# Value blocks as sequences of their own, and the first two sums of the last decoder as a piece of their own

## What is computed

```
# layer 0
xn = layernorm(x)
x = x + channel_attention(xn) + experts(xn)      # 64 experts, top 8, and a shared one
# layer 1
xn = layernorm(x)
x = x + sparse_attention(xn) + bitlinear_ffn(xn)

def sparse_attention(x):                         # per head h of 8, width 16
    q_h = relu(x @ enc_q[h]);  v_h = relu(x @ enc_v[h])
    metric = softplus(base + 0.1 * (gelu(signal(q) @ w1 + b1) @ w2 + b2))
    # each query looks at the 64 tokens up to itself
    dist = sqrt(((k_window - q_h) ** 2 * metric).sum(-1) + 1e-8)
    topd, loc = top_k(-dist, 32)
    infl = exp(-topd);  infl /= infl.sum() + 1e-8
    context = einsum(infl, v_h[loc])
    context += gate * 0.1 * (q_h / norm(q_h)) @ (hebb_U[h] @ hebb_V[h])
    return (q_h * context for all h) @ decoder
```

## Time and profile before

| | us |
|---|---|
| median of 3 runs (680.79 to 680.95) | 680.8 |
| the profiled execution | 682.07 |
| its span | 680.3 |
| PE busy | 642.2 (94%) |
| DVE busy | 550.7 (81%) |
| ACT busy | 444.3 (65%) |
| POOL busy | 367.6 (54%) |
| mean granted clock of TensorE | 0.988 |

### The profile page before, as it was taken

The page is one execution under the profiler, slowest core; times in us unless marked ns, Lnnn a source line. Parts: engine busy times, 40 slices in busy tenths (PEclk is TensorE's granted clock), DMA queues, the critical chain, the costliest instruction groups (busy, mean ns, idle before and its releaser), DMA issues.

```text
span 680.3 us, 14252 instructions
## 1 busy us (share of the span) xinstructions
PE 642.2 (94%) x4792; PEld 435.5 (64%) x4792; DVE 550.7 (81%) x2461; ACT 444.3 (65%) x802; POOL 367.6 (54%) x448
## 2 busy tenths in 40 slices
PE   4888999999999999999999999999999999998785
PEld 3555765667556666766666567666657766675674
DVE  5998688746967999997986999984477999937996
ACT  3675454646687868557688877446879855478762
POOL 2288366646363688755463895665653577511220
PEclk9999899999999899999999999999999999999898
DMA  8930000000000000000000000000000000000000
GB/s 299 402 116 1 0 1 0 1 0 1 0 1 1 2 2 1 1 1 1 2 0 2 2 2 1 1 1 1 1 1 2 2 1 1 1 17 2 18 17 17
DMA packets 12968, 15.81 MB, mean 23 GB/s; under 512 B 1728, under 2 KB 10832, under 8 KB 12384
## 3 DMA queue, kind: packets, MB, share of 16 engines
q1 hardware_dynamic: 12896, 14.91, 6.3%
HBM read 13.85 MB, written 1.05 MB: 22 GB/s over the span
## 4 chain that ended last, share of the span: by engine, by line
PE 70%; DVE 18%; ACT 5%; POOL 3%; issue 3%; DMA 0%; DVEq 0%; POOLq 0%; ACTq 0%
PE bank_A L523 19%; PE bank_G L523 16%; PE bank_U L523 16%; PE bank_X L523 16%; DVE Wk L1269 4%; DVE m L1266 3%; DVE S L850 2%; DVE GWk L850 2%; PE bank_X L816 1%; PE bank_X L532 1%; ACT Ed L1336 1%; ACT L1341 1%; POOL PR L1643 1%; POOL Wlo L1643 1%; ACT L1336 1%
## 5 line engine op out<-in xcount | busy, mean ns | idle before, releaser
L1643 POOL TENSOR_TENSOR Wlo<-Wgu,Whi 128x256 fp32r<-128x256 f32 x184 | 136.2, 747 | 135.1 <-ACT Whi L1336 134.3
L523 PE MATMUL bank_A<-S,WdT 128*128 128x512 f32 x346 | 171.4, 598 | 0.2 <-POOL S L1643 0.2
L850 DVE TENSOR_TENSOR S<-S,bank_U 128x512 f32<-128x512 f32 x173 | 116.6, 682 | 35.1 <-PE bank_U L523 21.3
L1643 POOL TENSOR_TENSOR S<-S,Rb 128x512 f32<-128x512 f32 x84 | 109.3, 1302 | 56.4 <-DVE S L850 55.9
L523 PE MATMUL bank_G<-xH,Whi 128*128 128x512 f32 x184 | 99.6, 541 | 4.5 <-POOL Wlo L1643 2.3
L1336 ACT ACTIVATE Whi<-Wgu 128x256 fp32r<-128x256 f32 x184 | 73.4, 412 | 40.8 <-PE bank_U L523 36.1
L523 PE MATMUL bank_U<-xH,Whi 128*128 128x512 f32 x184 | 96.7, 525 | 0.1
L523 PEld LDWEIGHTS bank_A<-S,WdT 128*128 128x128 f32 x346 | 62.7, 190 | 33.9 <-issue 23.3
L1269 DVE MATCH_REPLACE8 Wk<-m,Wk 128x79 f32<-128x79 f32 x384 | 82.1, 225 | 0.0
L1336 ACT ACTIVATE S<-bank_G 128x512 f32<-128x512 f32 x90 | 53.6, 596 | 43.1 <-PE bank_G L523 37.9
L850 DVE TENSOR_TENSOR S<-Rb,bank_G 128x512 f32<-128x512 f32 x83 | 56.3, 679 | 25.6 <-ACT bank_G L1336 20.0
(11 more groups left out here) (294 smaller groups left out, 1184.9 us busy)
## 6 DMA issues: line engine op xcount, KB each, us to landing
Wgu<-in_Wgu SPq DMA_DIRECT2D x2, 2048.0 KB, 14.2
xs<-in_x SPq DMA_DIRECT2D x4, 256.0 KB, 6.0
wqk<-in_w_qkv SPq DMA_DIRECT2D x1, 1024.0 KB, 7.2
Wgu<-in_Wgu SPq DMA_DIRECT2D x1, 1024.0 KB, 8.9
out<-xs SPq DMA_DIRECT2D x3, 256.0 KB, 2.3
Wgu<-in_Wgu SPq DMA_DIRECT2D x1, 512.0 KB, 5.1
wout<-in_w_out SPq DMA_DIRECT2D x1, 512.0 KB, 7.7
wvT<-in_wvT SPq DMA_DIRECT2D x1, 512.0 KB, 8.5
```

The costliest lines, as they stand in the source:

```text
L523: return engine.matmul(dst, lhsT, rhs, start=start, stop=stop)
L850: return engine.tensor_tensor(dst, a, b, op)
L1643: return engine.tensor_tensor(dst, a, b, op)
```

## The change

**Value blocks.** V0 and V1 leave `head` on PE and on ACT and become sequences of their own, `values(b)`, with the letters k on PE and v on ACT. In the banks they stand behind pq: in X2 for the batches 0 to 2, in U1 for the last one. There is no other work in them than before.

**Decoder.** Of the four products of a decoder sum in the last batch the first two, x·ident and hq·dec, become steps of their own, `decode_early`, with the letter x on PE. They count up a semaphore `dec_x`, for which `decode` waits before its two cc products.

**Order.** The strings of PE, DVE, ACT and POOL are written anew nearly throughout. No matmul and no other instruction is added or taken away. Lines of the changed kernel stand one less (523 is 522) up to the first hunk of PE, and 9 to 11 more behind it.

```diff
@@ uses()
-        for what in ("v0", "v1"):
-            add("U1" if last else "X2", what, b)
         for what in ("bdq", "hbm"):
             add("U0" if last else "X2", what, b)
-        add("U1" if last else "X2", "pq", b)
+        for what in ("pq", "v0", "v1"):
+            add("U1" if last else "X2", what, b)
@@ tensor engine
+            def values(b):
+                yTb = yT_of(b)
                 for k in range(2):
                     yield
                     t = fill(f"v{k}", b)
...
@@ decode(b, i)
-                t, c, h = fill("dec", b, i), cc[i % 2], slice(128 * i, 128 * i + 128)
-                pe.wait_ge("hq", 1)
-                if i < FIRST:
-                    pe.wait_ge(empty(bank("mo", b)), nth("mo", b) + 1)
-                else:
-                    pe.wait_ge(empty(bank("ff2", b)), nth("ff2", b) + 1)
-                mm(t[:, 0:128], ident, xb(b)[:, i, :], True, False)
+                t, c = ps("dec", b, i), cc[i % 2]
+                pe.wait_ge("dec_x", i + 1)
                 u = 2 * i + 1 + (i == NT - 1)
                 pe.wait_ge(empty(bank("ctx", b, u)), nth("ctx", b, u) + 1)
-                mm(t[:, 0:128], hq[:, h], dec[:, :], False, False)
                 mm(t[:, 0:128], c[:, 0, :], dec[:, :], False, False)
                 mm(t[:, 0:128], c[:, 1, :], dec[:, :], False, True).then_inc(sems(full(bank("dec", b, i))), 1)
+
+            def decode_early(b):
+
+                for i in range(NT):
+                    yield
+                    t = fill("dec", b, i)
+                    pe.wait_ge("hq", 1)
+                    if i < FIRST:
+                        pe.wait_ge(empty(bank("mo", b)), nth("mo", b) + 1)
+                    else:
+                        pe.wait_ge(empty(bank("ff2", b)), nth("ff2", b) + 1)
+                    mm(t[:, 0:128], ident, xb(b)[:, i, :], True, False)
+                    mm(t[:, 0:128], hq[:, 128 * i:128 * i + 128], dec[:, :], False, False).then_inc(sems("dec_x"), 1)
@@ weave
-                  h=heads(), d=every(distances), t=every(turns))
+                  h=heads(), k=every(values), d=every(distances), t=every(turns), x=decode_early(B - 1))
```

More of the change, by code:

```diff
@@ L44 @@
     "pe":
[L45 to L49, removed]
@@ L726, in head @@
                 mm(t[:, :], encq[:, :], yTb[:, :]).then_inc(sems(full(bank("enc", b))), 1)
-                for k in range(2):
-                    yield
-                    t = fill(f"v{k}", b)
-                    pe.wait_ge(empty(bank("y", b)), nth("y", b) + 1)
-                    for i in range(NG // 2):
-                        at = 64 * (NG // 2 * k + i) - 64
-                        o = slice(128 * i, 128 * i + 128)
-                        if at < 0:
-                            mm(t[0:64, o], yTb[:, 0:1].to_broadcast([128, 64]), encv[:, :])
-                            mm(t[64:128, o], yTb[:, 0:64], encv[:, :])
-                        else:
-                            p = mm(t[:, o], yTb[:, at:at + 128], encv[:, :])
-                    p.then_inc(sems(full(bank(f"v{k}", b))), 1)
                 yield
@@ L768, in head @@
                 p.then_inc(sems(full(bank("pq", b))), 1)
+            def values(b):
+                yTb = yT_of(b)
+                for k in range(2):
+                    yield
+                    t = fill(f"v{k}", b)
+                    pe.wait_ge(empty(bank("y", b)), nth("y", b) + 1)
+                    for i in range(NG // 2):
+                        at = 64 * (NG // 2 * k + i) - 64
+                        o = slice(128 * i, 128 * i + 128)
+                        if at < 0:
+                            mm(t[0:64, o], yTb[:, 0:1].to_broadcast([128, 64]), encv[:, :])
+                            mm(t[64:128, o], yTb[:, 0:64], encv[:, :])
+                        else:
+                            p = mm(t[:, o], yTb[:, at:at + 128], encv[:, :])
+                    p.then_inc(sems(full(bank(f"v{k}", b))), 1)
             def distances(b):
@@ L1523, in head @@
                 act(ksq[:, :], kp[:, PADK:], ACT.Square).then_inc(sems("ksq"), 1)
-                for k in range(2):
-                    yield
-                    t = filled(f"v{k}", b)
-                    if b > 0:
-                        q = NG // 2 * k + NG // 2 - 1
-                        sc_.wait_ge(full(bank("ctx", b - 1, q)), nth("ctx", b - 1, q) + 1)
-                    emptied(act(V[:, NG // 2 * k:NG // 2 * k + NG // 2, :],
-                                t[:, :].rearrange("p (g c) -> p g c", g=NG // 2), ACT.Relu), f"v{k}", b)
                 yield
@@ L1564, in head @@
                     ACT.Copy).then_inc(sems("pk"), 1)
+            def values(b):
+                for k in range(2):
+                    yield
+                    t = filled(f"v{k}", b)
+                    if b > 0:
+                        q = NG // 2 * k + NG // 2 - 1
+                        sc_.wait_ge(full(bank("ctx", b - 1, q)), nth("ctx", b - 1, q) + 1)
+                    emptied(act(V[:, NG // 2 * k:NG // 2 * k + NG // 2, :],
+                                t[:, :].rearrange("p (g c) -> p g c", g=NG // 2), ACT.Relu), f"v{k}", b)
             def operands(b):
@@ L1634, in scalar_engine @@
             weave("act", x=highs(), e=silus(), m=sums(), y=every(route), s=every(spreads), c=scales(), u=setup(),
-                  a=every(attend), f=every(dense), h=every(head), o=every(operands), k=every(keys), n=every(near), g=every(gather), q=ends())
+                  a=every(attend), f=every(dense), h=every(head), v=every(values), o=every(operands), k=every(keys), n=every(near), g=every(gather), q=ends())
         def gpsimd_engine(engine):
```

54 lines of the change are left out of this document (30 added, 24 removed).

## The result

The changed kernel takes 679.4 us by the median of 22 runs (677.9 to 681.4), the kernel before, over its own 22 runs, 681.0 (678.9 to 683.3). The ratio is 0.998, with a 95% interval of 0.997 to 0.9989: faster by 0.2%, some 1.4 us, where 4.6 us (676.2) were forecast with 679.0 as the upper bound. The two profiled executions show more, 682.07 and 678.06 us. The granted clock tells most of it.

The account below looks back on a forecast made before the run. Bounds: PE in the expert loop, a cross-engine chain in the last batch's head, DVE in its top-k, then the last chain. Terms −3.75 −0.43 −0.5 −0.3 +0.4 = −4.6 off 680.8 gave 676.2 us, range 673.4 to 679.0.

Parts of the forecast that it names:

- A: Last products of the expert loop: turn 2.6 moves behind the last two downs, PE still does not wait; −0.45 us.
- B: Last sums up to the keys: the last batch's ln starts when its input is ready; −0.85 us more.
- E: Head of the last batch: V0 in its new place on PE, between PQ and the first distances, costs +0.6 us.
- F: End of the kernel: first decoder products done early, cc·dec takes the place of hq·dec; −0.43 us (0.2 to 0.65).
- G: Start: PE's wait for rq goes, the bank of expert 8's U limits the gain; −0.5 us (−1.0 to +0.5).
- H: Expert loop: fewer changes between kinds of matmul on PE, 151 instead of 157; −0.3 us.
- I: Batch 2: a new wait at decoder step 1.3, now close behind context 1.7; +0.4 us (0 to +1.0).
- C: Last batch's head, ksq to hidden layer hb: value blocks and join leave the way; −3.2 us more.
- D: Last batch's head, hbm to nm: HBM stands behind a dense group needing bank X0; +0.2 us.
- Rival 3: Batch 2: ACT's kp held for a Hebbian product, silu queued behind, PE waits; slower, 682.2 us or more; chance 0.04.
- rival 1: PE's 3.4 us stretches at clock 0.50 shift: one more 677.9, one less in the loop 674.5 us; chance 0.17.

Follow-up runs that it names:

- the start alone: The kernel before with the changed order on all engines only up to expert 12, all else as before: 683.7 us, ratio 1.0041.

## Why the prediction was wrong, point by point

| term | forecast, us | in the traces |
|---|---|---|
| A, last products | −0.45 | −0.44 |
| B to E, head of the last batch | −3.30 | −3.87 |
| F, the last decoder sum | −0.43 | −0.39 |
| G, the start | −0.5 | +1.9 |
| H and I, the rest of the loop | +0.1 | +2.4 |

The right column adds up to −0.4. The ratio of the runs is worth −1.4, and so is the difference of the profiled pair with the two stretches of before taken off. In that pair 0.75 of the missing 1.0 lies behind the last Wm, over and above F, where the lower clock set in later after the change. The other 0.3 lies ahead of expert 7, a place that moves by as much between traces of one order.

**The tail was right, and rather too small.** A: PE did not wait on the last downs. B, C, D and E: −3.87 at the first MAX8 for −3.30; the values' part of it alone gave 1.1, the rest is join, dense pairs and turn. V0 in its place cost 0.61 for 0.6. The DVE stream took 50.8 us in both. F: 0.39 at equal clock, shown alone, for 0.43. Of the clock at the end the prediction has that it is at 1.2 GHz there. After the change it had fallen only at 674.0, with cc·dec ahead of it, and the stretch from cc to the end fell by 0.5 more than F in the profiled pair. The Trainium skill's rule ("TensorE: Matmul & The Clock Gate", What's actually happening), an array without work is run at the lower level, fits only roughly: 1.43 us of work in 5.10 at a mean of 0.78 here.

**G failed, and with it the sum.** It said −0.5, at worst +0.5, and it was +1.9 in the traces (+2.8 by the medians of the start alone, 1.8 to 3.7, with more of the lower clock in them). What it named was right: the wait for rq went, and one for U of expert 8 came, though of 1.1 and not below 0.5. The four xn stayed slow, 2.38 us at 39.59 with POOL beside them. The failed step is that I followed only the two engines of the row that I priced, DVE and PE, as far as expert 8. The new order had also moved the spreads on PE and the evictions Rb on ACT ahead of rq, and the chain behind rq, through ACT's PR, POOL's seven attention products and a low part of weights, comes to PE only at 57 us. That was 15 us behind the place where I stopped counting.

**H and I failed.** H gave −0.3 for fewer changes between kinds of matmuls. Nothing in the traces shows such a gain; as a term of its own it was not tested. I gave +0.4 for one wait that I had looked for; that one was 0.31. Together they should have been +0.1, and the loop behind expert 12 lost 2.4. It gained some 2 us up to 240 us, where I had left out the two waits that go, and lost over 4 behind. About 3 of these are seen as waits on PE of 0.2 to 0.7, most of them for DVE; the rest is spread over many distances and isn't traced. The failed step is that the loop was priced by its changes of kind and by one new wait, with DVE's lateness from 240 us on put at nothing. Rival 3 had this mechanism, a jam where engines are late and PE waits, but as one of 7 us at one place with a chance of 0.04. I had taken PE's idle time of before (4.7 us) as a bound on such losses; it bounds nothing in a new order.

**The clock** (rival 1) was real and is why one trace a side misleads. It put each stretch at 1.7; they cost 0.7 to 1.6. It does not explain the miss: with the two stretches of before taken off, the profiled pair differs by 1.4 us and not by 4.6.

## What to carry to other kernels

A new order of a whole program is many edits. Each place where it changes must be followed to the engine that bounds the time, across the queues of all engines: what stands behind a step that now waits is as much a part of its price as the step. If orders can be cut at a border and joined, cut them there. Two runs, old front with new tail and the reverse, told tail and loop apart, and three more found a join that beats both kernels (673.4 against 680.6 and 679.4). But look for waits that the join itself makes, like that of 1.0 us at 257. And where an engine is full, putting one small step forward can merely rename the wait.

## What was not expected of the hardware

The stretches at 0.50 fall on an array at work: the earlier trace rows has PE busy 3.30 of 3.30 us. The traces of these kernels have none to three of them in the loop, each 3.4 us long and often near the same times (74, 224 to 228, 369 to 371, and 623 to 644 us in the tail). They did not cost the same. Counted from expert 12 on, against a trace of the same order without one, that at 74 us cost 1.6 us, that at 224 to 228 some 1.2, and that at 370 some 0.7. Apart from them two traces of the same order agree within 0.3 us over 530. Over the runs of one kernel a lower mean granted clock goes with a longer time: four runs of the changed kernel at 0.996 took 677.9 to 678.1, and nine at 0.991 took 679.1 to 680.7. A median of 22 runs carries the stretches as scatter of 4 us between the fastest and the slowest.
